# Layer 0 of a two-layer graph attention: four chunks of a tile's probabilities transposed by DMA instead of three

## The chip, the cores and the metric

The kernel runs on one core of a Trainium2 chip. The metric is the device time of one execution in microseconds (us), the median of the runs of the kernel. In the profile the engines are PE (TensorE's matmuls; PEld are its weight loads), DVE (VectorE), ACT (ScalarE), POOL (GpSimd) and SP (SyncE, which here only issues DMAs).

## The reference

Two attention layers over 6144 rows of width 128, each followed by a residual sum and a layer norm. The change is in the first of them, called layer 0 in the reference and here.

```
def _L0_gnn_ref(xx_anchor, input, adj, weight):
    anchor_adj = jnp.einsum('md,de,ne->mn', xx_anchor, weight, input)
    scores = jnp.where(adj > 0, anchor_adj, NEG_PAD)
    atten = jax.nn.softmax(scores / TEMPERATURE, axis=1)
    return atten @ input

x = _layernorm(x + _L0_gnn_ref(x, L0_gnn_input, adj, L0_gnn_weight), axis=-1)
x = _layernorm(x + _L1_gnn_ref(x, adj, L1_gnn_W, L1_gnn_a1, L1_gnn_a2), axis=-1)
```

`adj` is an int32 matrix of 6144 x 6144, `input` and `x` are float32 matrices of 6144 x 128. Layer 1 uses the same `adj` with additive scores and does not touch what is changed.

## The kernel before

**Tiles and steps.** Layer 0 works through 48 tiles of 128 rows. A tile has 6144 columns, cut in 12 chunks of 512. The kernel is a software pipeline: iteration `t` has 12 steps `c` = 0 to 11, and at step `c` the engines work on chunks of three tiles. In iteration `t`, PE makes the scores of chunk `c` of tile `t` (three matmuls of 512 columns, L574 to L576, since the operands are split into a high and a low float16 part). DVE adds the mask and keeps the maximum, a pair of chunks at a time, at odd steps (L866). ACT takes the exponential of chunk `c` of tile `t - 1` (L730). PE turns a chunk of probabilities with four float32 transposes (L563) three steps after its exponential, ACT rounds the turned chunk to float16 (`pT_hi`, L717), DVE subtracts for the low part (`pT_lo`, L875), and PE multiplies both with `vals` two steps later (L541, L543, eight matmuls). PSUM has two banks for turned chunks, so a turn waits until `pT_lo` of the turn but one before has been made; a scores matmul at an even step waits for the masked pair of three steps before.

**The moved chunks.** The first `MOVED` = 3 chunks of each tile are not turned by PE. ACT rounds them in one copy to float16 (`moved_hi`, L724, at step `c == MOVED`), POOL subtracts for the low part in one instruction (`moved_lo`, L429), and SP issues one DMA transpose for each (L352, L354). PE uses them last of the tile, in the next iteration. In the profile `moved_hi` and `moved_lo` carry the name `inp_sb`, whose space they take over. So the steps of an iteration at which a moved chunk's turn would stand (3, 4, 5) have no transposes.

**Masks.** The adjacency of a tile comes in four quarters of 1536 columns. DVE turns each into a mask `neg_mask` of zeros and large negative numbers (`make_mask`, L841); quarters 0 and 1 of tile `t + 1` are made at steps 6 and 8 of iteration `t`, quarters 2 and 3 of tile `t` at steps 0 and 2 of iteration `t`. From each mask POOL makes a byte mask for layer 1 (`edges`, L404), which SP stores. The adjacency loads of the next tile wait for the masks.

**What sets the order.** Every engine runs its instructions in the order in which the code emits them, and waits on semaphores. POOL's order in an iteration is written out in `tile_rstd`: `edges` of quarter 2, `score_cols` (two instructions on an earlier tile's result, L415 and L421), `edges` of quarter 3, `moved_lo`, `edges` of quarters 0 and 1 of the next tile, and a small power (L447). ACT adds up the product of `score_cols` at step 4 (L696), ahead of its exponential of step 5 and of `xT_hi` (L685), the rounding of the next tile's transposed rows, from which DVE makes `xT_lo` (L832).

Of the kernel before, what the change touches and what calls it, by code (L numbers as in the profile page):

```python
# [9 lines left out]
LAG = 3  # L10
PT_SLOTS = 4
PV_LAG = 2
MOVED = 3
PARTS = 8
PART_SLOTS = 4
Z_LEAD = 2
# [21 lines left out]
def build(nc, x, adj, inp, w0, w1, a1, a2, edge_rows, out):  # L38
# [17 lines left out]
    with ExitStack() as ctx:  # L56
# [37 lines left out]
        pT_lo = sb0("pT_lo", [P, PT_SLOTS, CHUNK], F16)  # L94
        MW = MOVED * CHUNK
        inp_space = inp_sb[:].bitcast(F16).rearrange("p b d -> p (b d)")
# [118 lines left out]
        vals_lo = sem("vals_lo")  # L215
# [44 lines left out]

        TURNS = C - MOVED
        ATT_STEP = LAG + PV_LAG + MOVED

# [4 lines left out]
        def turn_number(tile, bc):  # L268
            return TURNS * tile + bc - MOVED

# [7 lines left out]
        def movedT_loads(tile):  # L278
            return 32 * (tile // 2 + 1)
# [6 lines left out]
        def scores_of(known):  # L286
            return known is None or known < NB
# [19 lines left out]
        def _(sp):  # L307
# [22 lines left out]
            def load_tile(t, par, known):  # L330
                if scores_of(known) and known != 0:

                    after(sp, x_turned, t)
                    sp.dma_start(xq[:], pair_rows(x, t)).then_inc(xq_in, 16)
                    for q in range(QUARTERS):

                        after(sp, mask_set, QUARTERS * (t - 1) + q + 1)
                        sp.dma_start(adj_sb[:, q, :], pair_rows(adj, t)[:, q * QW:(q + 1) * QW]).then_inc(adj_in[q], 16)
                        store_edges(t - 1, q)
                        if q == 1 and t >= 2:  # L340
                            load_xr(t - 2)
                if t == NB:
                    for q in range(QUARTERS):
                        store_edges(t - 1, q)
                    load_xr(t - 2)
                if 2 <= t <= NB + 1:
                    tile = t - 2
                    sp.wait_ge(moved_hi_set, tile + 1)
                    if tile < 2:
                        sp.wait_ge(vals_lo, (6, 9)[tile])  # L350
                    after(sp, pv_done, C * (tile - 1))
                    sp.dma_start_transpose(movedT[:, par, 0], moved_hi).then_inc(movedT_in[par], 16)  # L352
                    sp.wait_ge(moved_lo_set, tile + 1)
                    sp.dma_start_transpose(movedT[:, par, 1], moved_lo).then_inc(movedT_in[par], 16)  # L354
                if t == NB + 1:
                    load_xr(t - 2)
# [28 lines left out]
        def _(pool):  # L385
# [37 lines left out]
            def moved_low(tile):  # L423
                pool.wait_ge(moved_hi_set, tile + 1)
                if tile == 0:
                    pool.wait_ge(vals_lo, 3)
                if tile >= 1:
                    pool.wait_ge(movedT_in[(tile - 1) % 2], movedT_loads(tile - 1))
                nc.gpsimd.tensor_tensor(moved_lo, rows[:, tile % 2 * N:tile % 2 * N + MOVED * CHUNK], moved_hi,  # L429
                                        ALU.subtract).then_inc(moved_lo_set, 1)  # L430
# [238 lines left out]
        def _(act):  # L669
# [29 lines left out]
            def tile_steps(t, par, known):  # L699
                for c in range(C):  # L700
                    if known == 0:
                        if c + Z_LEAD + 1 < C:
                            inpT_out(c + Z_LEAD + 1)
                        if c + Z_LEAD < C:
                            z_high(c + Z_LEAD)
                    if c == ATT_STEP and ends_tile(known):

                        act.wait_ge(pv_done, C * (t - 1))
                        after(act, u_set, t - 2)
                        nc.scalar.copy(att[:], ps[:, PV, 0:2 * P]).then_inc(att_out, 1)  # L710
                    if turn_at(known, c):
                        off, bc = turn_of(t, c)
                        n = turn_number(t - off, bc)
                        act.wait_ge(turned, n + 1)
                        if n >= PT_SLOTS:
                            act.wait_ge(pv_done, attend_number((n - PT_SLOTS) // TURNS, (n - PT_SLOTS) % TURNS + MOVED) + 1)
                        nc.scalar.copy(pT_hi[:, n % PT_SLOTS, :], ps[:, PT0 + n % NPT, :]).then_inc(pT_hi_set, 1)  # L717
                    if c == MOVED and 1 <= t <= NB:
                        act.wait_ge(exp_set, C * (t - 1) + MOVED)
                        if t == 1:  # L720
                            act.wait_ge(vals_lo, 3)
                        if t >= 2:
                            act.wait_ge(movedT_in[t % 2], movedT_loads(t - 2))
                        nc.scalar.copy(moved_hi, rows[:, (1 - par) * N:(1 - par) * N + MOVED * CHUNK]).then_inc(moved_hi_set, 1)  # L724
                    if known is None or 1 <= known <= NB:

                        if c == 0:
                            act.wait_ge(bias_set, t)
                            after(act, sum_set, t - 2)
                        nc.scalar.activation(row_chunk(1 - par, c), row_chunk(1 - par, c), ACT.Exp,  # L730
                                             bias=exp_bias[:, 1 - par:2 - par], scale=EXP_SCALE,
                                             accum_out=part_sum[:, 1 - par, c:c + 1]).then_inc(exp_set, 1)
                    if c == x_step(known) and (known is None or known < NB - 1):
                        xT_high(t + 1, 1 - par)
                    if c == 4 and t >= 3:
                        score_sums(t - 3)
# [76 lines left out]
        def _(dve):  # L813
# [21 lines left out]
            def make_mask(t, q, known):  # L835

                dve.wait_ge(adj_in[q], 16 * (t + 1))

                after(dve, masked, PAIRS * (t - 1) + pairs_of(q) if known != 0 else 0)
                after(dve, edges_set, QUARTERS * (t - 1) + q + 1 if known != 0 else 0)  # L840
                nc.vector.tensor_scalar(neg_mask[:, q, :], adj_sb[:, q, :], 0.0, -MASK_BIG, ALU.is_le,  # L841
                                        ALU.mult).then_inc(mask_set, 1)
# [6 lines left out]
            def tile_steps(t, par, known):  # L849
                for c in range(C):  # L850
# [27 lines left out]
                    if known == 0:  # L878
                        if c in (2, 5, 8):
                            make_mask(0, c // QC + 1, 0)  # L880
                        elif c >= C - 2:
                            make_mask(1, c - (C - 2), None)
                    else:
                        if c in (0, 2) and scores_of(known):
                            make_mask(t, 2 + c // 2, known)
                        if c in (6, 8) and (known is None or known < NB - 1):
                            make_mask(t + 1, (c - 6) // 2, None)
                    if t == 0 and c >= 5 and c % 2 == 1:
# [186 lines left out]
```

## Time and profile before

| | us |
|---|---|
| median of 3 runs | 1493.58 |
| lowest and highest | 1492.31, 1494.48 |
| the profiled execution's own time | 1494.69 |
| its span | 1492.9 |
| PE busy in the span | 1439.6 (96%) |
| DVE busy | 1326.4 (89%) |
| ACT busy | 1065.3 (71%) |
| POOL busy | 982.8 (66%) |
| DMA engines' share (the main queue) | 70.3% |

The span runs from the first to the last instruction that the profiler saw. Busy times are unions over an engine's instructions; PE's matmuls overlap, so that a busy PE says only that it did not stand still. Layer 0 takes about the first 1010 us of the span; its 48 tiles follow one another at equal distances.

### The profile page before, as it was taken

What the parts mean: (1) busy time and instruction counts of PE and PEld (TensorE: products, weight loads), DVE (VectorE), ACT (ScalarE), POOL (GpSimd) and SP (SyncE); (2) the same over time, 40 slices, a digit from 0 to 9 for tenths busy, and PEclk for the clock granted to TensorE, in tenths of its full rate; (3) what the DMA queues carried; (4) which work ended last, traced back from release to release, by engine and by line L of the source; (5) the groups of instructions that cost most, each with busy time, mean ns of one, the idle gap of its engine ahead of it and who ended that gap; (6) DMA issues with size and microseconds to landing.
All of it is one profiled execution on the core that took longest, in us unless ns stands there. A gap on an engine that the chain in (4) does not pass through costs nothing.

```text
span 1492.9 us, 28265 instructions
## 1 busy us (share of the span) xinstructions
PE 1439.6 (96%) x9853; PEld 1030.7 (69%) x9853; DVE 1326.4 (89%) x2303; ACT 1065.3 (71%) x2327; POOL 982.8 (66%) x629
## 2 busy tenths in 40 slices
PE   7799999999999999999999999987999999999996
PEld 4477777777777777777777777774566666666664
DVE  5999999999999999999999999967779797979794
ACT  4588888888888888888888888877745454546463
POOL 6455555555555555555555555527999999999995
PEclk9999999999999999999999999998999999999998
DMA  7889889888898889899989888753334343444420
GB/s 253 241 236 257 232 241 257 246 241 235 250 260 238 238 243 254 240 238 251 255 235 244 245 256 231 195 114 86 85 64 100 84 99 84 98 86 94 90 57 14
DMA packets 378766, 278.81 MB, mean 187 GB/s; under 512 B 307713, under 2 KB 354049, under 8 KB 378625
## 3 DMA queue, kind: packets, MB, share of 16 engines
q1 hardware_dynamic: 378624, 277.01, 70.3%
q8 instruction: 79, 1.29, 0.4%
q14 instruction: 63, 0.51, 0.1%
HBM read 160.56 MB, written 40.89 MB: 135 GB/s over the span
## 4 chain that ended last, share of the span: by engine, by line
PE 90%; POOL 3%; DVE 2%; issue 2%; ACT 1%; DMA 1%; SPq 0%; ACTq 0%; POOLq 0%; DVEq 0%
PE ps L541 16%; PE ps L563 13%; PE ps L623 11%; PE ps L616 10%; PE ps L543 8%; PE ps L574 8%; PE ps L576 8%; PE ps L575 8%; PE ps L600 5%; POOL p_lo L460 2%; PE ps L634 1%; DMA inp_sb<-inp 1%; ACT rows L730 1%; POOL vals_lo L456 1%; DVE rows L866 1%
## 5 line engine op out<-in xcount | busy, mean ns | idle before, releaser
L404 POOL TENSOR_SCALAR edges<-neg_mask 128x1536 uint8<-128x1536 bf16 x192 | 285.0, 1484 | 329.3 <-DVE neg_mask L841 329.0
L730 ACT ACTIVATE rows<-rows,exp_bias 128x512 f32<-128x512 f32 x576 | 415.2, 721 | 40.5 <-DVE exp_bias L933 40.5
L460 POOL TENSOR_TENSOR p_lo<-p,p_hi 128x1024 fp32r<-128x1024 f32 x180 | 426.5, 2408 | 13.2 <-PE ps L600 7.7
L960 DVE SCALAR_TENSOR_TENSOR p<-ps,e_col,edgesT 128x1024 f32<-128x1024 f32 x288 | 349.0, 1277 | 62.2 <-PE ps L593 37.5
L866 DVE CUSTOM_DVE_ANT_0 rows<-ps,neg_mask 128x1024 f32<-128x1024 f32 x288 | 351.1, 1219 | 32.3 <-PE ps L576 26.0
L717 ACT CAST pT_hi<-ps 128x512 f16<-128x512 f32 x432 | 252.1, 583 | 135.7 <-PE ps L563 127.7
L541 PE MATMUL ps<-vals,pT_hi 128*128 128x256 f16 x1728 | 331.8, 273 | 1.2 <-ACT att L710 0.8
L759 ACT CAST p_hi<-p 128x1024 fp32r<-128x1024 f32 x180 | 185.1, 1047 | 176.6 <-DVE p L960 174.4
L543 PE MATMUL ps<-vals,pT_lo 128*128 128x128 f16 x1728 | 308.6, 219 | 0.0
L875 DVE TENSOR_TENSOR pT_lo<-ps,pT_hi 128x512 f16<-128x512 f32 x432 | 287.8, 684 | 17.3 <-ACT pT_hi L717 17.3
L563 PE MATMUL ps<-ident,rows 128*128 128x128 f32 x1728 | 263.6, 275 | 7.4 <-DVE pT_lo L875 6.4
L574 PE MATMUL ps<-zT,xT_hi 128*128 128x512 f16 x576 | 219.5, 381 | 5.8 <-DVE part_max L866 4.0
L575 PE MATMUL ps<-zT,xT_hi 128*128 128x512 f16 x576 | 219.3, 381 | 0.0
L576 PE MATMUL ps<-zT,xT_lo 128*128 128x512 f16 x576 | 219.3, 381 | 0.0
L841 DVE TENSOR_SCALAR neg_mask<-adj_sb 128x1536 bf16<-128x1536 int32 x192 | 218.4, 1137 | 0.0
L541 PEld LDWEIGHTS ps<-vals,pT_hi 128*128 128x128 f16 x1728 | 169.2, 98 | 66.2 <-DVE pT_lo L875 1.9
L543 PEld LDWEIGHTS ps<-vals,pT_lo 128*128 128x128 f16 x1728 | 169.2, 98 | 49.6 <-issue 0.3
L623 PE MATMUL ps<-p,vals 128*128 128x512 f32 x432 | 203.5, 593 | 0.0
L563 PEld LDWEIGHTS ps<-ident,rows 128*128 128x128 f32 x1728 | 184.8, 142 | 19.2 <-issue 6.4
L616 PE MATMUL ps<-p_hi,vals_hi 128*128 128x512 f32 x360 | 157.3, 518 | 7.6 <-POOL vals_lo L456 5.0
L429 POOL TENSOR_TENSOR inp_sb<-rows,inp_sb 128x1536 f16<-128x1536 f32 x48 | 149.8, 3120 | 6.5 <-ACT inp_sb L724 2.7
L623 PEld LDWEIGHTS ps<-p,vals 128*128 128x128 f32 x432 | 81.4, 189 | 60.6 <-issue 52.2
(108 smaller groups left out, 1731.0 us busy)
## 6 DMA issues: line engine op xcount, KB each, us to landing
adj_sb<-adj SPq DMA_DIRECT2D x192, 768.0 KB, 5.3
edge_rows<-edges SPq DMA_DIRECT2D x192, 192.0 KB, 4.8
xq<-x SPq DMA_DIRECT2D x48, 64.0 KB, 2.6
xr<-x SPq DMA_DIRECT2D x48, 64.0 KB, 1.9
out<-y_w SPq DMA_DIRECT2D x5, 512.0 KB, 3.7
inp_sb<-inp SPq DMA_DIRECT2D x3, 768.0 KB, 10.1
inp_sb<-inp_sb SPq DMA_TRANSPOSE x96, 5.1
edgesT<-edge_rows SPq DMA_TRANSPOSE x48, 5.6
```

The source lines that it names most:

```text
L460: nc.gpsimd.tensor_tensor(p1_lo[:, m % LO_SLOTS, :], p1[:, (NB * g + n) % P_SLOTS, :], p1_hi[:, m % HI_SLOTS, :].bitcast(F32), ALU.subtrac ...
L541: nc.tensor.matmul(acc, p_hi, vals[:, jb, :], start=(bc == MOVED and b == 0), stop=False, skip_group_check=True)
L543: mm = nc.tensor.matmul(acc[:, P:2 * P], p_lo, vals[:, jb, 0:P], start=False, stop=(bc == MOVED - 1 and b == BPC - 1), skip_group_check=True)
L563: mm = nc.tensor.transpose(ps[:, PT0 + n % NPT, b * P:(b + 1) * P], rows[:, pb * N + bc * CHUNK + b * P:pb * N + bc * CHUNK + (b + 1) * P] ...
L574: nc.tensor.matmul(scores_bank(c), xT_hi[:, par, :], zT[:, 0, cols], start=True, stop=False)
L575: nc.tensor.matmul(scores_bank(c), xT_hi[:, par, :], zT[:, 1, cols], start=False, stop=False)
L576: nc.tensor.matmul(scores_bank(c), xT_lo[:, par, :], zT[:, 0, cols], start=False, stop=True).then_inc(scored, 1)
L616: mm = nc.tensor.matmul(acc_half(g % 2, i), v[:, k, :], p1_hi[:, m % HI_SLOTS, i * CHUNK:(i + 1) * CHUNK], start=(n == 0 and v is vals1_hi ...
L623: mm = nc.tensor.matmul(acc_half(g % 2, i), vals1[:, n, :], p1[:, (NB * g + n) % P_SLOTS, i * CHUNK:(i + 1) * CHUNK], start=(n == 0), stop ...
L730: nc.scalar.activation(row_chunk(1 - par, c), row_chunk(1 - par, c), ACT.Exp, bias=exp_bias[:, 1 - par:2 - par], scale=EXP_SCALE, accum_ou ...
L866: nc.vector.tensor_tensor_reduce(row_pair(par, k), scores_pair(k), neg_mask_row[:, 2 * k * CHUNK:2 * (k + 1) * CHUNK], 1.0, -3.0e38, ALU.a ...
L960: nc.vector.scalar_tensor_tensor(out=p1[:, (NB * g + n) % P_SLOTS, :], in0=ps[:, R_ROW:R_ROW + 2, :].rearrange("p b w -> p (b w)"), scalar ...
```

## The change

`MOVED` goes from 3 to 4: chunks 0 to 3 of each tile take the way over DMA, and PE has 8 chunks to turn instead of 9. `moved_hi` and `moved_lo` grow from 1536 to 2048 columns; the ACT copy stands at step 4 instead of 3. `ATT_STEP` (the step from which a tile's products with `vals` begin) is `LAG + PV_LAG + MOVED` and goes from 8 to 9, and with it go the copy of the finished sums (L710) and the small instructions of the layer norm on DVE (L908 to L921). The counts that guard the shared space of `inp_sb` are adapted. Apart from that, `make_mask` of quarters 2 and 3 stands at steps 2 and 4 instead of 0 and 2.

```diff
-MOVED = 3
+MOVED = 4
...
                     if tile < 2:
-                        sp.wait_ge(vals_lo, (6, 9)[tile])
+                        sp.wait_ge(vals_lo, MOVED * (tile + 2))
...
                 if tile == 0:
-                    pool.wait_ge(vals_lo, 3)
+                    pool.wait_ge(vals_lo, MOVED)
...
                         if t == 1:
-                            act.wait_ge(vals_lo, 3)
+                            act.wait_ge(vals_lo, MOVED)
...
-                        if c in (0, 2) and scores_of(known):
-                            make_mask(t, 2 + c // 2, known)
+                        if c in (2, 4) and scores_of(known):
+                            make_mask(t, 1 + c // 2, known)
                         if c in (6, 8) and (known is None or known < NB - 1):
                             make_mask(t + 1, (c - 6) // 2, None)
```

DVE's queue before, in steps 0 to 5 of an iteration (`x_all` is the finished row of an earlier tile; L866 is a pair of scores, its second row the reading of the maximum; the masks are quarters 2 and 3):

```order
L841 TENSOR_SCALAR neg_mask<-adj_sb 128x1536 [waits edges_set,masked,adj_in2]
L924 TENSOR_SCALAR x_all<-xr,moments,small 128x128 [waits rstd_set]
L866 ISA rows,part_max<-ps,neg_mask 128x1024 [waits max_set,scored,moved_lo_set,mask_set]
L866 ISA part_max 128x1
L875 TENSOR_TENSOR pT_lo<-ps,pT_hi 128x512 [waits pT_hi_set] x2
L841 TENSOR_SCALAR neg_mask<-adj_sb 128x1536 [waits edges_set,masked,adj_in3]
L866 ISA rows,part_max<-ps,neg_mask 128x1024 [waits turned,scored,moved_lo_set,mask_set]
L866 ISA part_max 128x1
L897 TENSOR_REDUCE small<-part_sum 128x1
L899 RECIPROCAL small<-small 128x1 [waits sum_set]
L866 ISA rows,part_max<-ps,neg_mask 128x1024 [waits scored,turned,mask_set]
```

The same place now:

```order
L924 TENSOR_SCALAR x_all<-xr,moments,small 128x128 [waits rstd_set]
L866 ISA rows,part_max<-ps,neg_mask 128x1024 [waits max_set,scored,moved_lo_set,mask_set]
L866 ISA part_max 128x1
L875 TENSOR_TENSOR pT_lo<-ps,pT_hi 128x512 [waits pT_hi_set] x2
L841 TENSOR_SCALAR neg_mask<-adj_sb 128x1536 [waits edges_set,masked,adj_in2]
L866 ISA rows,part_max<-ps,neg_mask 128x1024 [waits scored,moved_lo_set,mask_set]
L866 ISA part_max 128x1
L897 TENSOR_REDUCE small<-part_sum 128x1
L899 RECIPROCAL small<-small 128x1 [waits sum_set]
L841 TENSOR_SCALAR neg_mask<-adj_sb 128x1536 [waits edges_set,masked,adj_in3]
L866 ISA rows,part_max<-ps,neg_mask 128x1024 [waits scored,turned,mask_set]
```

The mask of quarter 2 has moved behind the pair of step 1 and the two `pT_lo` of steps 1 and 2; the one of quarter 3 stands behind the pair of step 3 and the two small instructions, where it meets the pair of step 5.

DVE's queue right behind, from the end of step 5's pair to step 8, before (the masks are quarters 0 and 1 of the next tile):

```order
L866 ISA part_max 128x1
L832 SCALAR_TENSOR_TENSOR xT_lo<-ps,xT_hi 128x128 [waits xT_hi_set]
L902 TENSOR_SCALAR small<-small 128x1 [waits inv_set]
L875 TENSOR_TENSOR pT_lo<-ps,pT_hi 128x512 [waits pT_hi_set]
L841 TENSOR_SCALAR neg_mask<-adj_sb 128x1536 [waits edges_set,masked,adj_in0]
L866 ISA rows,part_max<-ps,neg_mask 128x1024 [waits scored,turned,mask_set]
L866 ISA part_max 128x1
L875 TENSOR_TENSOR pT_lo<-ps,pT_hi 128x512 [waits pT_hi_set] x2
L841 TENSOR_SCALAR neg_mask<-adj_sb 128x1536 [waits edges_set,masked,adj_in1]
```

The same place now:

```order
L866 ISA part_max 128x1
L832 SCALAR_TENSOR_TENSOR xT_lo<-ps,xT_hi 128x128 [waits xT_hi_set]
L902 TENSOR_SCALAR small<-small 128x1 [waits inv_set]
L841 TENSOR_SCALAR neg_mask<-adj_sb 128x1536 [waits edges_set,masked,adj_in0]
L866 ISA rows,part_max<-ps,neg_mask 128x1024 [waits scored,turned,mask_set]
L866 ISA part_max 128x1
L875 TENSOR_TENSOR pT_lo<-ps,pT_hi 128x512 [waits pT_hi_set] x2
L841 TENSOR_SCALAR neg_mask<-adj_sb 128x1536 [waits edges_set,masked,adj_in1]
```

The `pT_lo` of step 6 is gone from between the small instruction and the mask of quarter 0.

POOL's queue in an iteration, from the `edges` of quarter 2, before:

```order
L404 TENSOR_SCALAR edges<-neg_mask 128x1536 [waits mask_set,edges_out2]
L415 TENSOR_TENSOR s_prod<-x_all,wa_rep 128x256 [waits s_set,wa_copied,x1_set]
L421 TENSOR_TENSOR x_total<-x_total,x_all 128x128 [waits total_set]
L404 TENSOR_SCALAR edges<-neg_mask 128x1536 [waits mask_set,edges_out3]
L429 TENSOR_TENSOR inp_sb<-rows,inp_sb 128x1536 [waits movedT_in1,moved_hi_set]
L404 TENSOR_SCALAR edges<-neg_mask 128x1536 [waits mask_set,edges_out0]
L404 TENSOR_SCALAR edges<-neg_mask 128x1536 [waits mask_set,edges_out1]
```

The same place now:

```order
L404 TENSOR_SCALAR edges<-neg_mask 128x1536 [waits mask_set,edges_out2]
L415 TENSOR_TENSOR s_prod<-x_all,wa_rep 128x256 [waits s_set,wa_copied,x1_set]
L421 TENSOR_TENSOR x_total<-x_total,x_all 128x128 [waits total_set]
L404 TENSOR_SCALAR edges<-neg_mask 128x1536 [waits mask_set,edges_out3]
L429 TENSOR_TENSOR inp_sb<-rows,inp_sb 128x2048 [waits movedT_in1,moved_hi_set]
L404 TENSOR_SCALAR edges<-neg_mask 128x1536 [waits mask_set,edges_out0]
L404 TENSOR_SCALAR edges<-neg_mask 128x1536 [waits mask_set,edges_out1]
```

Only the width of the subtraction L429 has changed in POOL's queue, from 1536 to 2048; what has moved is when the masks come that its `edges` wait for.

## Rows read from the trace of the kernel before

**Rows 1.** Busy time by stretch, 42 tiles of layer 0: engine busy us (instructions).

```profile
core 0: us, PE busy (x) PEld busy (x) DVE busy (x) ACT busy (x) POOL busy (x), PEclk, DMA share, GB/s
132.89:969.45 836.56, 836.35 (x7100) 625.62 (x7098) 795.54 (x1555) 688.41 (x1681) 449.62 (x337) 1.00 0.89 243
```

**Rows 2.** Timeline, PE, one tile: start us, us, engine, line, xcount.

```profile
500.18 0.61 PE L563 MATMUL ps<-ident,rows 128*128 128x128 f32 x4
...
501.94 0.61 PE L563 MATMUL ps<-ident,rows 128*128 128x128 f32 x4
...
510.81 0.38 PE L574 MATMUL ps<-zT,xT_hi 128*128 128x512 f16 x1
...
512.12 0.38 PE L574 MATMUL ps<-zT,xT_hi 128*128 128x512 f16 x1
```

**Rows 3.** Timeline, DVE, the same tile, [idle before <- releaser].

```profile
507.90 0.95 DVE L841 TENSOR_SCALAR neg_mask<-adj_sb 128x1536 bf16<-128x1536 int32 x1
...
511.37 1.16 DVE L841 TENSOR_SCALAR neg_mask<-adj_sb 128x1536 bf16<-128x1536 int32 x1
512.45 1.21 DVE L866 CUSTOM_DVE_ANT_0 rows<-ps,neg_mask 128x1024 f32<-128x1024 f32 x1
...
513.78 0.16 DVE L899 RECIPROCAL small<-small 128x1 f32<-128x1 f32 x1
514.41 1.23 DVE L866 CUSTOM_DVE_ANT_0 rows<-ps,neg_mask 128x1024 f32<-128x1024 f32 x1 [0.47 <-PE ps L576]
...
515.56 0.29 DVE L832 SCALAR_TENSOR_TENSOR xT_lo<-ps,xT_hi 128x128 f16<-128x128 f32 x1
515.76 0.14 DVE L902 TENSOR_SCALAR small<-small 128x1 f32<-128x1 f32 x1
...
516.71 1.46 DVE L841 TENSOR_SCALAR neg_mask<-adj_sb 128x1536 bf16<-128x1536 int32 x1
518.09 1.21 DVE L866 CUSTOM_DVE_ANT_0 rows<-ps,neg_mask 128x1024 f32<-128x1024 f32 x1
...
519.23 1.28 DVE L875 TENSOR_TENSOR pT_lo<-ps,pT_hi 128x512 f16<-128x512 f32 x2
520.43 0.94 DVE L841 TENSOR_SCALAR neg_mask<-adj_sb 128x1536 bf16<-128x1536 int32 x1
```

**Rows 4.** Timeline, POOL, the same tile.

```profile
510.57 0.73 POOL L415 TENSOR_TENSOR s_prod<-x_all,wa_rep 128x256 f32<-128x256 f32 x1
511.25 0.46 POOL L421 TENSOR_TENSOR x_total<-x_total,x_all 128x128 f32<-128x128 f32 x1
512.69 1.47 POOL L404 TENSOR_SCALAR edges<-neg_mask 128x1536 uint8<-128x1536 bf16 x1 [0.98 <-DVE neg_mask L841]
514.24 3.11 POOL L429 TENSOR_TENSOR inp_sb<-rows,inp_sb 128x1536 f16<-128x1536 f32 x1
```

**Rows 5.** Timeline, ACT, the same tile.

```profile
511.03 1.47 ACT L724 CAST inp_sb<-rows 128x1536 f16<-128x1536 f32 x1
...
513.83 0.29 ACT L696 ACTIVATE s_prod<-s_prod 128x128 f32<-128x128 f32 x1
...
515.12 0.26 ACT L685 ACTIVATE xT_hi<-ps 128x128 f16<-128x128 f32 x1
```

**Rows 6.** Timeline, POOL, near the start.

```profile
43.98 1.77 POOL L404 TENSOR_SCALAR edges<-neg_mask 128x1536 uint8<-128x1536 bf16 x1 [0.97 <-DVE neg_mask L841]
```

**Rows 7.** Timeline, DVE, near the start.

```profile
43.74 0.67 DVE L827 SCALAR_TENSOR_TENSOR vals<-inp_sb,vals 128x512 f16<-128x512 f32 x1
...
44.63 1.93 DVE L841 TENSOR_SCALAR neg_mask<-adj_sb 128x1536 bf16<-128x1536 int32 x1
```

**Rows 8.** Timeline, SP's queue, the tile of rows 3.

```profile
514.93 2.48 SPq L352 DMA_TRANSPOSE inp_sb<-inp_sb  x1
517.47 2.42 SPq L354 DMA_TRANSPOSE inp_sb<-inp_sb  x1
```

**Rows 9.** The page's DMA issues: xcount, us to landing.

```profile
inp_sb<-inp_sb SPq DMA_TRANSPOSE x96, 5.1
```

## The prediction

> **What bounds the kernel now.** I read the busy times of the long even stretch of layer 0 first, then one tile of it on each engine. 42 tiles take 836.56 us, 19.92 us each, at PE's full granted clock (1.00, the 2.4 GHz level) [rows 1]. PE stands still for only 0.2 us of all that, so PE bounds layer 0. But DVE is busy 795.54 us, 18.94 of 19.92 us per tile, and hardly has room. ACT has 3.5 us per tile to spare, POOL 9.2, and the DMA engines show a share of 0.89 [rows 1]. PE's timeline gives its prices: a step with a turn takes 501.94 - 500.18 = 1.76 us, one without 512.12 - 510.81 = 1.31 us [rows 2]. A turn costs 0.45 us.
>
> On DVE some masks are stretched. The same instruction takes 0.95, 1.16, 1.46 and 0.94 us [rows 3]. The two long ones start while POOL runs: `x_total` ends at 511.71 and `moved_lo` at 517.35 [rows 4], and the masks end at 512.53 and 518.17 [rows 3], each 0.82 us after POOL. So such a mask does next to nothing until POOL's instruction ends. POOL's `edges` does the same to it: one runs from 43.98 to 45.75 [rows 6], and the mask started at 44.63 ends at 46.56 [rows 7], 0.81 us later. It holds the other way too: that `edges` took 1.77 us instead of 1.47 [rows 4, 6] since DVE's low part of `vals` was running until 44.41 when it started [rows 7]. Whoever starts first keeps the other out. No mask of the tile shown was running when a POOL instruction started, so for this pair the second direction is inferred.
>
> The Trainium skill, page "SBUF — State Buffer", section "SBUF: two separate sides", says that DVE and GpSimd share a pair of ports under an exclusive lock, held by the one that starts first for its whole instruction. The rows above agree.
>
> **The change, part by part.**
>
> PE loses one turn per tile, 0.45 us. If nothing else held, a tile would take 19.92 - 0.45 = 19.5 us, and the kernel 48 x 0.45 = 21.6 us less: 1473 against the profiled execution's own 1494.69.
>
> DVE loses one `pT_lo`. Two take 520.43 - 519.23 = 1.20 us [rows 3], so 0.60. Without it and without the stretching (0.21 + 0.51) DVE's work is 18.94 - 0.60 - 0.72 = 17.6 us per tile. What decides is how much of the 19.5 - 17.6 = 1.9 us between them the collisions with POOL take.
>
> `moved_lo` takes 3.11 us for 1536 columns [rows 4]; from 128 columns (0.46) to 1536 the slope is 1.9 ns per column, so 2048 cost 4.1 us. `moved_hi` on ACT goes from 1.47 us [rows 5] to 1.96 at most, by a third, and a rounding of a turned chunk goes away: no price, since ACT has 3.5 us per tile.
>
> I walk DVE and POOL through the new order. Time 0 is the start of quarter 2's mask. Prices on DVE, start to start [rows 3]: mask 0.87 free, or 0.74 after POOL lets go; pair 1.14; reduction and reciprocal 0.35; `xT_lo` 0.20 and the small one 0.14; `pT_lo` 0.60. On POOL: `edges` starts 0.16 after its mask's end and takes 1.47, `s_prod` and `x_total` 1.14 together, 0.08 between two [rows 3, 4].
>
> - POOL's `edges` of quarter 2 runs from 1.11 to 2.58. DVE reaches quarter 3's mask at 2.36, is held until 2.58, goes on at 3.32. `s_prod`, due at 2.67, finds that mask running and ends at 4.0, `x_total` at 4.45; `edges` of quarter 3 runs from 4.5 to 6.0.
> - ACT adds up `s_prod` ahead of its exponential of step 5 and of `xT_hi`: start of the sums to start of `xT_hi` is 515.12 - 513.83 = 1.29 us, and `xT_hi` takes 0.26 [rows 5]. So `xT_hi` ends at 5.6. DVE, done with its pair at 4.46, waits for it, and reaches quarter 0's mask at 6.0 instead of 4.8. This mask ends its slot at 6.8.
> - `moved_lo` is due at 6.06, finds the mask running, and runs from 6.75 to 10.85. Before, it was over 517.35 - 511.37 = 5.98 us after quarter 3's mask had begun; now 8.5.
> - DVE makes a pair and two `pT_lo` and reaches quarter 1's mask at 9.14. It is held until 10.85 and leaves at 11.59.
>
> Without collisions this part of DVE's queue takes 4 masks, 3 pairs, 2 `pT_lo` and 0.69: 8.8 us. It takes 11.6: 2.8 us are lost. The rest of the tile is 17.6 - 8.8 = 8.8 us. Sum: 20.4. In that rest the two updates of `xr`, which read two operands from SBUF as the low part of `vals` does, meet POOL's delayed `edges` of quarter 1: 0.6 us more by the same walk (bounds 0 and 1.5, one whole `edges`). Sum: 21.0 us per tile, 1.1 more than 19.92. PE, with 19.5, waits for `pT_lo`: the turn of step 11 needs the one of step 9, which now comes behind the mask held longest. Over 45 tiles that is +50 us; the three others and the tail keep their 0.45: -1. Against the profiled execution's own 1494.69 us (span 1492.9) this gives 1544, and against the median, 1.1 lower, **1542 us**.
>
> The other things that move are hidden. The layer norm's instructions on DVE go one step back; the power on POOL and the exponential's bias come some 0.6 us later, and ACT has that room. The loads of quarters 2 and 3 start two steps later and are needed two steps later. The transposes: SP's issue takes 2.4 to 2.5 us each [rows 8], a third more now; before, the second was issued at 517.47 and landed about 5.1 us later [rows 9], 522.6, and PE needs it at step 5 of the next tile, 513.4 + 19.9 = 533.3 [rows 2]. Some 6 us later still fits. Adjacency loads queued behind them on SP are needed a tile later. The DMA engines: 0.89 of 19.92 is 17.7 us of work per tile, 243 GB/s x 19.92 us = 4.84 MB, of which the moved transposes are 0.79. A third more of these is 0.95 us by bytes, 1.9 if they cost double: 19.6 us at most, under DVE's time.
>
> **The rivals.**
>
> PE stays the bound (faster). It takes a POOL that is not held up by running masks, against the second direction above: the walk's POOL chain then ends 1.45 us earlier, DVE's tile comes to 19.6 with the `xr` updates and 19.0 without, PE's is 19.5. Time: 1473. Against it: the low part of `vals` does hold POOL; and 1.9 us of room against 2.8 needed.
>
> The collisions are short (no change or a little slower). If `s_prod` does not hold up ACT and only one of the two masks delays POOL, 19.9 to 20.3 us per tile: 1493 to 1511.
>
> `moved_lo` wins the race against quarter 0's mask (much slower). They come at 6.06 and 6.0, closer than I can read the walk. The mask would then be held until 10.16, the pair of step 7 start at 10.9, quarter 1's mask run freely to 14.1 and a tile take 23.5 us: 45 x 3.6 = +162, 1655. It decides from a mask 0.06 us later. If it wins in some tiles only, the time lies between. For the mask: it waits already when `edges` ends, while POOL needs 0.08 us to its next.
>
> The transfers become the bound: 19.6 us at most by the bytes, inside the first rival.
>
> **How the numbers follow.** The forecast mechanism, 1511 to 1575: 0.52. The race lost in part or wholly, 1575 to 1660: 0.2. Short collisions, 1497 to 1511: 0.08, and 1490 to 1497: 0.05. PE the bound, 1473: 0.12. Worse than 1660: 0.03. The range 1497 to 1660 holds 0.8. A measurement tells 0.2% (3 us) from no change. Faster by more: 0.13. Within it: 0.04. Slower: 0.83, by the same cases.
>
> **What would show it.** Right: steps without turns are four per tile; `moved_lo` is 4.1 us long; quarter 1's masks take about 2.5 us instead of 0.94 and end 0.8 after `moved_lo`; DVE waits for `xT_hi`; PE waits for `pT_lo` at a turn; tiles 21 us apart. Quarter 0's masks of 5 us would show the lost race. Wrong: masks all near 0.95 us and PE without gaps at 19.5 us per tile, or POOL instructions that start under a running mask and keep their usual length.

## The result

The changed kernel takes 1535.48 us (median of 4 runs, 1534.76 to 1537.93) against 1494.03 us of the kernel before (4 runs, 1492.31 to 1494.64): 1.0283 times as long, 95% interval 1.0267 to 1.0298. The forecast was 1542 us, in a range of 1497 to 1660. The profiled execution took 1534.76 us with a span of 1532.7 us, 39.8 us longer than the span before.

The busy times of the long even stretch of layer 0, in the columns of [rows 1], now read (span 1532.7 us):

```profile
132.89:969.45 836.56, 793.09 (x6642) 581.82 (x6641) 787.21 (x1450) 648.95 (x1570) 542.22 (x322) 1.00 0.88 247
```

PE, which had no gaps in [rows 1], stands still for 43.5 of 836.56 us. The turns it no longer makes have turned into waiting, and into more of it. POOL's busy time has grown from 449.62 to 542.22 us in the same stretch, though it now holds 40 tiles instead of 42; the 40 longer `moved_lo` account for 40 x 1.0 us. DMA share (0.88 for 0.89) and granted clock stay where they were.

One tile on DVE, the timeline that answers to [rows 3] (start, length, engine, line, operation; idle time before it in brackets):

```profile
509.12 0.95 DVE L841 TENSOR_SCALAR neg_mask<-adj_sb 128x1536 bf16<-128x1536 int32 x1
...
511.44 1.08 DVE L841 TENSOR_SCALAR neg_mask<-adj_sb 128x1536 bf16<-128x1536 int32 x1
...
514.73 0.29 DVE L832 SCALAR_TENSOR_TENSOR xT_lo<-ps,xT_hi 128x128 f16<-128x128 f32 x1 [1.05 <-ACT xT_hi L685]
...
515.00 0.95 DVE L841 TENSOR_SCALAR neg_mask<-adj_sb 128x1536 bf16<-128x1536 int32 x1
...
517.00 1.28 DVE L875 TENSOR_TENSOR pT_lo<-ps,pT_hi 128x512 f16<-128x512 f32 x2
518.20 2.51 DVE L841 TENSOR_SCALAR neg_mask<-adj_sb 128x1536 bf16<-128x1536 int32 x1
520.63 1.21 DVE L866 CUSTOM_DVE_ANT_0 rows<-ps,neg_mask 128x1024 f32<-128x1024 f32 x1
...
522.98 0.75 DVE L908 SCALAR_TENSOR_TENSOR xr<-att,small,xr 128x128 f32<-128x128 f32 x1
...
529.90 0.95 DVE L841 TENSOR_SCALAR neg_mask<-adj_sb 128x1536 bf16<-128x1536 int32 x1
```

Two masks of quarter 2 start at 509.12 and 529.90: a tile takes 20.78 us instead of 19.92. The mask of quarter 1 at 518.20 takes 2.51 us, where it took 0.94 in [rows 3]. DVE waits 1.05 us for `xT_hi`.

POOL in the same tile, answering to [rows 4]:

```profile
511.79 1.31 POOL L415 TENSOR_TENSOR s_prod<-x_all,wa_rep 128x256 f32<-128x256 f32 x1
...
515.15 4.74 POOL L429 TENSOR_TENSOR inp_sb<-rows,inp_sb 128x2048 f16<-128x2048 f32 x1
519.98 3.62 POOL L404 TENSOR_SCALAR edges<-neg_mask 128x1536 uint8<-128x1536 bf16 x2
```

`moved_lo` ends at 515.15 + 4.74 = 519.89, and the held mask at 518.20 + 2.51 = 520.71, 0.82 us later, the same distance as in the kernel before. And here is what the trace of before did not have: POOL instructions that started while a mask was running. `s_prod` shows 1.31 us instead of 0.73, and `moved_lo` 4.74 us, against 4.09 where it starts beside no mask (run a below). The two `edges` at 519.98 show the same once more: `moved_lo` has ended, the held mask is running, and the first of the two takes 2.06 us instead of 1.47. Together POOL is held 1.8 us per tile (0.58, 0.65 and 0.59).

Not every DVE instruction is held. In the stretch above, 120 pairs of scores and 200 `pT_lo`, which read one operand from PSUM, started while a POOL instruction was running and had 0.2 us or more to go, and kept their usual length (1.21 to 1.23 and 0.67 to 0.69 us). Held were the masks (1.08 and 2.51 us) and the first update of `xr` (0.75 instead of 0.34 us).

PE in the same tile, with the wait that the profile puts to it:

```profile
519.61 0.61 PE L563 MATMUL ps<-ident,rows 128*128 128x128 f32 x4
...
522.60 0.63 PE L563 MATMUL ps<-ident,rows 128*128 128x128 f32 x4 [1.08 <-DVE pT_lo L875]
```

From one turn to the next it is 2.99 us instead of 1.76. The turn at 522.60 (step 11) waits 1.08 us for `pT_lo` of step 9, which DVE makes behind the held mask and a pair of scores.

### The profile page after: what moved, and what is told of

It reads as the page before. It is cut to its first block, busy times and chain, and to the rows that moved or that the text cites. A ratio compares the mean times of both kernels' runs of the same rounds, so it can differ in the third digit from the quotient of the medians.

```text
span 1532.7 us, 27643 instructions
## 1 busy us (share of the span) xinstructions
PE 1430.0 (93%) x9661; PEld 1010.4 (66%) x9661; DVE 1353.4 (88%) x2255; ACT 1051.8 (69%) x2279; POOL 1112.6 (73%) x629
## 4 chain that ended last, share of the span: by engine, by line
DVE 38%; PE 30%; issue 13%; POOL 11%; ACT 5%; POOLq 0%; ACTq 0%; DVEq 0%
DVE pT_lo L875 12%; DVE rows L866 12%; PE ps L623 11%; PE ps L616 10%; DVE neg_mask L841 7%; PE ps L600 5%; POOL edges L404 4%; POOL s_prod L415 4%; POOL p_lo L460 2%; ACT rows L730 2%; DVE xr L908 2%; ACT s_prod L696 2%; PE ps L541 1%; PE ps L634 1%; DVE x_all L924 1%
## 5 line engine op out<-in xcount | busy, mean ns | idle before, releaser
L404 POOL TENSOR_SCALAR edges<-neg_mask 128x1536 uint8<-128x1536 bf16 x192 | 311.5, 1622 | 212.0 <-DVE neg_mask L841 200.6
L866 DVE CUSTOM_DVE_ANT_0 rows<-ps,neg_mask 128x1024 f32<-128x1024 f32 x288 | 351.3, 1220 | 6.7 <-PE ps L576 6.5
L717 ACT CAST pT_hi<-ps 128x512 f16<-128x512 f32 x384 | 222.2, 579 | 143.9 <-PE ps L563 143.6
L541 PE MATMUL ps<-vals,pT_hi 128*128 128x256 f16 x1536 | 295.3, 273 | 1.3 <-ACT att L710 0.8
L563 PE MATMUL ps<-ident,rows 128*128 128x128 f32 x1536 | 235.9, 276 | 57.5 <-DVE pT_lo L875 56.0
L543 PE MATMUL ps<-vals,pT_lo 128*128 128x128 f16 x1536 | 274.7, 219 | 0.0
L841 DVE TENSOR_SCALAR neg_mask<-adj_sb 128x1536 bf16<-128x1536 int32 x192 | 265.1, 1381 | 0.3 <-POOL edges L404 0.3
L875 DVE TENSOR_TENSOR pT_lo<-ps,pT_hi 128x512 f16<-128x512 f32 x384 | 250.7, 682 | 9.7 <-ACT pT_hi L717 9.6
L429 POOL TENSOR_TENSOR inp_sb<-rows,inp_sb 128x2048 f16<-128x2048 f32 x48 | 226.0, 4708 | 7.6 <-ACT inp_sb L724 3.9
L563 PEld LDWEIGHTS ps<-ident,rows 128*128 128x128 f32 x1536 | 162.5, 142 | 79.6 <-issue 71.8
L541 PE MATMUL ps<-vals,inp_sb 128*128 128x256 f16 x768 | 146.9, 273 | 0.0
```

The source lines that it names most:

```text
L404: nc.gpsimd.tensor_scalar(edge_bytes[:, q, :], neg_mask[:, q, :], 1.0 / MASK_BIG, 1.0, ALU.mult, ALU.add).then_inc(edges_set, 1)
L541: nc.tensor.matmul(acc, p_hi, vals[:, jb, :], start=(bc == MOVED and b == 0), stop=False, skip_group_check=True)
L543: mm = nc.tensor.matmul(acc[:, P:2 * P], p_lo, vals[:, jb, 0:P], start=False, stop=(bc == MOVED - 1 and b == BPC - 1), skip_group_check=True)
L563: mm = nc.tensor.transpose(ps[:, PT0 + n % NPT, b * P:(b + 1) * P], rows[:, pb * N + bc * CHUNK + b * P:pb * N + bc * CHUNK + (b + 1) * P] ...
L866: nc.vector.tensor_tensor_reduce(row_pair(par, k), scores_pair(k), neg_mask_row[:, 2 * k * CHUNK:2 * (k + 1) * CHUNK], 1.0, -3.0e38, ALU.a ...
L875: nc.vector.tensor_tensor(pT_lo[:, s, :], ps[:, PT0 + n % NPT, :], pT_hi[:, s, :], ALU.subtract).then_inc(pT_lo_set, 1)
```

## The walk against the trace

The prediction's sum was a walk through DVE's and POOL's queues from the start of quarter 2's mask. The same points in the trace of after, less 509.12:

| point | walk | trace |
|---|---|---|
| DVE reaches the mask of quarter 3 | 2.36 | 2.32 |
| it goes on behind it | 3.32 | 3.33 |
| `s_prod` ends | 4.0 | 3.98 |
| `xT_hi` ends | 5.6 | 5.57 |
| the mask of quarter 0 starts | 6.0 | 5.88 |
| DVE goes on behind it | 6.8 | 6.74 |
| `moved_lo` is due | 6.06 | 6.03 |
| `moved_lo` ends | 10.85 | 10.77 |
| DVE reaches the mask of quarter 1 | 9.14 | 9.08 |
| it goes on behind it | 11.59 | 11.51 |
| the delay of the `xr` updates | 0.6 | 0.4 |
| the tile | 21.0 | 20.78 |

## Experiments

The theory: a mask on DVE and POOL's instructions shut each other out, and this, not the transfers, the longer copy or the number of turns, took the time. The rivals: the DMA transposes of a third more data (the DMA engines or SP's queue); ACT's longer copy; DVE's wait for `xT_hi`; and, for the way to PE, whether it is DVE's whole sum or one `pT_lo` that comes too late.

The runs in one view (each in turn below; "after" is the changed kernel):

| | moved chunks | masks of quarters 2, 3 / 0, 1 at steps | else | us |
|---|---|---|---|---|
| before | 3 | 0, 2 / 6, 8 | | 1494 |
| after | 4 | 2, 4 / 6, 8 | | 1535 |
| c | 4 | 2, 4 / 6, 8 | POOL subtracts a quarter | 1475 |
| d | 4 | 2, 4 / 6, 8 | transposes of 3 chunks | 1534 |
| a | 4 | 0, 2 / 6, 8 | | 1559 |
| b | 3 | 2, 4 / 6, 8 | | 1671 |
| g | 4 | 2, 4 / 6, 8 | sums behind `xT_hi` | 1531 |
| h | 4 | 2, 4 / 6, 8 | `pT_lo` first | 1558 |
| j | 4 | 0, 2 / 6, 8 | `pT_lo` first | 1523 |
| e | 4 | 0, 2 / 4, 8 | | 1496 |
| f | 4 | 0, 2 / 4, 8 | `pT_lo` first | 1469 |
| i | 3 | 0, 2 / 4, 8 | `pT_lo` first | 1489 |

### c: POOL's subtraction cut short

```diff
-nc.gpsimd.tensor_tensor(moved_lo, rows[:, tile % 2 * N:tile % 2 * N + MOVED * CHUNK], moved_hi,
+nc.gpsimd.tensor_tensor(moved_lo[:, :CHUNK], rows[:, tile % 2 * N:tile % 2 * N + CHUNK], moved_hi[:, :CHUNK],
...
-sp.dma_start_transpose(movedT[:, par, 1], moved_lo)
+sp.dma_start_transpose(movedT[:, par, 1], moved_hi)
```

> The changed kernel with POOL's subtraction cut to 512 of its 2048 columns (left out: the low part of three of the four moved chunks; the second transpose of full size reads moved_hi instead). Port theory: moved_lo takes about 1.2 us and is over before quarter 1's mask comes; of the held time only xT_hi's 1.1 us and 0.1 stay, DVE needs 18.9 us, under PE's 19.5, and the kernel is at 1473 to 1480 us. If the transfers or the ACT copy were the cost, it stays near 1535.

Measured: 1475.45 us, 0.9881 of before (0.9866 to 0.9896). The stretch of layer 0, same columns (span 1473.5):

```profile
132.89:969.45 836.56, 835.11 (x7073) 619.25 (x7071) 761.45 (x1540) 689.69 (x1672) 424.13 (x341) 1.00 0.92 257
```

PE is without gaps again, the tile takes 19.52 us (two masks of quarter 2 at 519.20 and 538.72), and that with all the transfers and the long copy of the changed kernel: the DMA share is even higher, 0.92. One instruction of POOL was shortened (and the second transpose reads `moved_hi`, at full size), and 60 us are gone. `xT_hi`'s wait of 1.05 us is still there 31 times in 600 us and costs nothing.

### d: the transposes cut short

```diff
-sp.dma_start_transpose(movedT[:, par, 0], moved_hi)
+sp.dma_start_transpose(movedT[:, par, 0, 0:12], moved_hi[:, 0:12 * P])
...
-p_hi = movedT[:, t_of % 2, 0, jb, :] if by_dma else pT_hi[:, s, cols]
+p_hi = movedT[:, t_of % 2, 0, jb % 12, :] if by_dma else pT_hi[:, s, cols]
```

(and the same for the low part)

> The changed kernel with both DMA transposes cut to three of the four chunks (left out: the transposed fourth chunk; PE reads the first one's blocks in its place). Everything on the engines is as in the changed kernel. Port theory: no difference to the changed kernel, 1535 us within 3. Transfer theory (DMA engines or SP's queue the bound): back to the transfers of before and so PE's 19.5 us per tile, 1473 to 1490.

Measured: 1534.3 us (1533.71 to 1535.01), 1.0274 of before (1.0259 to 1.029). The DMA share fell from 0.88 to 0.80 and the time by 1 us. The transfers have no part in the loss.

### a: four moved chunks, masks where they were

```diff
-                        if c in (2, 4) and scores_of(known):
-                            make_mask(t, 1 + c // 2, known)
+                        if c in (0, 2) and scores_of(known):
+                            make_mask(t, 2 + c // 2, known)
```

> Four moved chunks, but the masks of quarters 2 and 3 at steps 0 and 2 as before. Port theory (a DVE mask and a POOL instruction shut each other out): moved_lo starts some 2.9 us after quarter 3's mask and runs 4.1 us, so quarter 0's mask at step 6 comes under it and is held about 2.3 us, while quarter 1's is free; DVE's tile is 17.6 + 2.5 held + up to 0.5 of waiting = 20.1 to 20.6 us, the kernel 1502 to 1525 us, likeliest 1513. If the moving of the masks were the whole cost, this kernel would show PE's gain: 1473. If the longer transfers or the longer ACT copy were the cost, it would stay at 1535.

Measured: 1559.15 us, 1.0441 of before (1.0425 to 1.0457). The direction of the port theory, but 46 us more than its likeliest value and outside its interval. DVE's timeline, the held mask; POOL's, `moved_lo` with no mask running when it starts; and PE's, the turn that waited (span 1558.0):

```profile
506.04 3.43 DVE L841 TENSOR_SCALAR neg_mask<-adj_sb 128x1536 bf16<-128x1536 int32 x1
509.39 1.21 DVE L866 CUSTOM_DVE_ANT_0 rows<-ps,neg_mask 128x1024 f32<-128x1024 f32 x1
...
510.53 1.28 DVE L875 TENSOR_TENSOR pT_lo<-ps,pT_hi 128x512 f16<-128x512 f32 x2
```

```profile
504.56 4.09 POOL L429 TENSOR_TENSOR inp_sb<-rows,inp_sb 128x2048 f16<-128x2048 f32 x1
```

```profile
511.36 0.63 PE L563 MATMUL ps<-ident,rows 128*128 128x128 f32 x4 [1.75 <-DVE pT_lo L875]
```

The mask was held as computed (3.43 us instead of 0.95, so 2.5). What the expectation left out is the way to PE: `pT_lo` of step 7 stands behind the held mask and the pair, and the turn of step 9 needs it. The expectation had added up DVE's work; the tile is 21.3 us since PE stood still 1.75 us for one late `pT_lo`, and then DVE waited for PE's scores in its turn (20.2 us busy of 21.3, the held time counted as busy).

### b: three moved chunks, masks moved

```diff
-                        if c in (0, 2) and scores_of(known):
-                            make_mask(t, 2 + c // 2, known)
+                        if c in (2, 4) and scores_of(known):
+                            make_mask(t, 1 + c // 2, known)
```

(the change to the kernel before)

> Three moved chunks as before, only the masks of quarters 2 and 3 at steps 2 and 4. Port theory: moved_lo (3.1 us) is due about 6.1 us after quarter 2's mask starts; quarter 0's mask now has a pT_lo ahead of it and comes at 6.5, so it loses the race and is held till 9.2; with the wait for xT_hi (1.2 us) DVE's tile is 18.2 + 0.1 + 1.2 + 2.6 = 22.1 us, the kernel about 1590 us (1560 to 1610), slower than with four moved chunks. If four moved chunks were the cost (their transfers, the longer copy), this kernel would be at 1494, and at 1473 + 21 = 1494 too if the masks' place did not matter.

Measured: 1671.03 us, 1.1184 of before (1.1165 to 1.1202). The slowest of all, with PE's and the transfers' work of the kernel before. Its mask of quarter 0 loses the race that the changed kernel's wins. DVE, then POOL, then PE (span 1669.3):

```profile
505.88 0.69 DVE L875 TENSOR_TENSOR pT_lo<-ps,pT_hi 128x512 f16<-128x512 f32 x1
506.49 3.28 DVE L841 TENSOR_SCALAR neg_mask<-adj_sb 128x1536 bf16<-128x1536 int32 x1
```

```profile
505.84 3.11 POOL L429 TENSOR_TENSOR inp_sb<-rows,inp_sb 128x1536 f16<-128x1536 f32 x1
```

```profile
511.66 1.09 PE L563 MATMUL ps<-ident,rows 128*128 128x128 f32 x4 [2.68 <-DVE pT_lo L875]
512.54 0.63 PE L574 MATMUL ps<-zT,xT_hi 128*128 128x512 f16 x1
```

`moved_lo` started 0.65 us ahead of the mask; DVE went on at 509.69. The expectation had the hold and its place, and 81 us too little, outside its interval. Most of what it lacked is the clock. PE's granted clock in the wait, right behind it and after that (columns as in [rows 1]):

```profile
508.90:511.66 2.76, 0.08 (x3) 0.03 (x1) 2.76 (x5) 0.31 (x2) 1.52 (x2) 0.99 0.94 181
511.66:515.06 3.40, 3.40 (x15) 2.26 (x16) 2.17 (x3) 1.30 (x3) 1.47 (x1) 0.51 0.95 237
515.06:524.10 9.04, 9.04 (x79) 6.87 (x78) 7.99 (x21) 6.54 (x16) 0.56 (x1) 1.00 0.41 155
```

Behind the stretch without matmuls the granted clock is 0.51, the 1.2 GHz level: the four transposes take 1.09 us instead of 0.61, a scores matmul 0.63 instead of 0.38. The run itself has the comparison: through the long stretch, four tiles of five have such a time at half clock and take 24.0 to 24.3 us; every fifth has none, at the same wait of 2.68 us, and takes 22.76. So the low clock costs 1.2 to 1.6 us in a tile that has it, 1.1 on the mean of all, and the mean tile is 23.9 us, 1.8 more than the expected 22.1. The other 0.7 us stand in the tiles at full clock too; DVE waits there 0.49 us for PE's scores at step 1, which the expectation had not in its sum, and the rest was not followed up. In the changed kernel, with waits of 1.08 us, and in a, with 1.75, the mean over the stretch is 1.00.

### g: the sums behind `xT_hi`

```diff
-                    if c == 4 and t >= 3:
+                    if c == 5 and t >= 3:
                         score_sums(t - 3)
```

> The changed kernel with ACT's sums of s_prod at step 5 behind xT_hi instead of at step 4. DVE's wait for xT_hi of 1.05 us per tile goes. Port theory: it changes nothing, since quarter 0's mask then comes 1.2 us earlier and is held by edges of quarter 3 until about the same time (5.95 us after quarter 2's mask started, measured now: it starts at 5.88): quarter 0's mask shows 1.9 to 2.2 us instead of 0.95, time 1535 within 4. If the wait for xT_hi were worth its length, 45 x 1.05 = 47 us less: 1488.

Measured: 1531.08 us (1530.36 to 1531.3), 1.0251 of before (1.0237 to 1.0265), 4.4 us less than the changed kernel, against 47 if the wait were worth its length. DVE's masks of quarters 0 and 1 (span 1529.2):

```profile
511.64 2.02 DVE L841 TENSOR_SCALAR neg_mask<-adj_sb 128x1536 bf16<-128x1536 int32 x1
...
515.93 2.49 DVE L841 TENSOR_SCALAR neg_mask<-adj_sb 128x1536 bf16<-128x1536 int32 x1
```

The wait of 1.05 us is gone and its place is taken by POOL's `edges`: the mask of quarter 0 now takes 2.02 us instead of 0.95; quarter 1's mask, at the end of the chain, takes 2.5 us as before. The wait for `xT_hi` was covered: the time is within the 4 us that the expectation allowed.

### h: `pT_lo` ahead of the pair, in the changed kernel

```diff
+                    if turn_at(known, c):
+                        ...
+                        nc.vector.tensor_tensor(pT_lo[:, s, :], ps[:, PT0 + n % NPT, :], pT_hi[:, s, :],
+                                                ALU.subtract).then_inc(pT_lo_set, 1)
                     if scores_of(known) and c % 2 == 1:
                         ...
-                    if turn_at(known, c):
-                        ...
```

> The changed kernel with pT_lo ahead of the pair of scores at odd steps on DVE. It asks how the held mask reaches PE. If by the turn of step 11, which waits 1.08 us for pT_lo of step 9 behind the pair (1.14 us), that wait ends, and what is left is DVE's own sum: 17.6 of work, 1.7 held by POOL in quarter 1's mask, 0.1 in quarter 3's, 0.4 in xr, 1.05 waiting for xT_hi, together 20.8, the same as measured: DVE alone is the bound and the time stays at 1525 to 1536. If PE's stall by the order of pT_lo is the bound and DVE is not, 45 x 1.08 = 49 us less: 1487.

Measured: 1557.94 us, 1.0431 of before (1.0416 to 1.0445): slower than either answer. The tile is 21.29 us, 0.51 more. On DVE there is one new wait, at step 1 (span 1554.9):

```profile
516.52 0.34 DVE L923 TENSOR_SCALAR x_all<-xr,moments,small 128x128 f32<-128x128 f32 x1
517.36 0.69 DVE L860 TENSOR_TENSOR pT_lo<-ps,pT_hi 128x512 f16<-128x512 f32 x1 [0.50 <-ACT pT_hi L717]
```

There DVE used to make the pair while ACT, held up by the late `exp_bias`, was still at `pT_hi`; now it stands 0.50 us, and the tile is longer by just that. Meanwhile PE's wait at step 11 went down from 1.08 to 0.71 us, and gained nothing; another of 0.57 us came up at the turn of step 2. So in the changed kernel DVE's chain is what closes: its work, what POOL holds it, and its waits; PE only follows. The expectation's first answer had this right and had not looked for what the swap costs at step 1. The swap changes the order at every odd step, so this run doesn't show what it is worth at step 9 alone.

### j: the same swap in a

The edit is h's, in a.

> a_masks_0_2 (1559 us, 21.3 us per tile) with pT_lo ahead of the pair at odd steps. In a, PE waits 1.75 us at the turn of step 9 for a pT_lo that stands behind the held mask and a pair, and DVE is busy 20.2 us per tile. If PE's local wait set a's time, the pair's 1.14 us come off and DVE's sum takes over, 20.2 us plus the 0.5 that h lost at step 1: 20.7, 1533 us (1520 to 1545). If DVE's sum had set it already, nothing changes or it is 0.5 us per tile slower as h was: 1558 to 1582.

Measured: 1522.99 us (1521.78 to 1523.6), 1.0192 of before (1.0177 to 1.0208), 36 us less than a, as expected for the case that PE's wait set a's time. The held mask is still 3.43 us; the tile went from 21.3 to 20.56 us. In a the late `pT_lo` did set the time, which is the term that a's expectation lacked.

### e: the mask of quarter 0 two steps earlier

```diff
-                        if c in (2, 4) and scores_of(known):
-                            make_mask(t, 1 + c // 2, known)
-                        if c in (6, 8) and (known is None or known < NB - 1):
-                            make_mask(t + 1, (c - 6) // 2, None)
+                        if c in (0, 2) and scores_of(known):
+                            make_mask(t, 2 + c // 2, known)
+                        if c in (4, 8) and (known is None or known < NB - 1):
+                            make_mask(t + 1, (c - 4) // 4, None)
```

> Four moved chunks, masks of quarters 2 and 3 at steps 0 and 2 as before, the next tile's quarter 0 at step 4 (before: 6), quarter 1 at 8. Port theory: quarter 0's mask starts ahead of moved_lo, at the end of POOL's edges (held 0.2 us), moved_lo follows it from about 0.7 us later and is over (4.1 us) when quarter 1's mask comes at step 8; held time 0.4 to 0.6 us, DVE 18.2 us per tile, PE the bound at 19.5: 1474 us (1470 to 1480), faster than both. If the turned chunk's saving were taken back by something else (transfers, ACT's longer copy), it would stay above 1490.

Measured: 1496.26 us, 1.0018 of before (1.0009 to 1.0027): 39 us less than the changed kernel, and still 22 above the expectation. DVE's masks, POOL's `edges` of quarter 0, and the turn that waited (span 1495.3):

```profile
515.48 1.08 DVE L841 TENSOR_SCALAR neg_mask<-adj_sb 128x1536 bf16<-128x1536 int32 x1
...
520.98 1.88 DVE L841 TENSOR_SCALAR neg_mask<-adj_sb 128x1536 bf16<-128x1536 int32 x1
```

```profile
515.83 4.67 POOL L429 TENSOR_TENSOR inp_sb<-rows,inp_sb 128x2048 f16<-128x2048 f32 x1
520.58 1.47 POOL L404 TENSOR_SCALAR edges<-neg_mask 128x1536 uint8<-128x1536 bf16 x1
```

```profile
504.83 0.63 PE L563 MATMUL ps<-ident,rows 128*128 128x128 f32 x4 [0.37 <-DVE pT_lo L875]
```

The races at steps 4 and 8 against `moved_lo` went as meant. But behind `moved_lo` comes the `edges` of quarter 0, which had been due since 516.7, and it starts 0.40 us ahead of the mask of quarter 1 and holds it for 1.07 us. The expectation followed the long instruction and forgot the one queued behind it. PE waits 0.37 us at the turn of step 11, which comes 2.29 us after the turn of step 10 (502.54) instead of 1.75, and the tile is 19.92 us. At 1496 the run also lies above the 1490 that the expectation gave to another cause, the transfers or ACT's longer copy taking the saving back. f, with the same transfers and the same copy, rules that out.

### f: both

e with h's swap.

> As e_mask_at_4, and DVE makes pT_lo of an odd step ahead of the step's pair of scores instead of behind it. PE is at its own work of 19.5 us per tile in e already, so this gives nothing: 1474 us within 3 of e. If e still has PE waiting for pT_lo, f takes that back (up to 0.2 us per tile, 9 us).

Measured: **1469.49 us** (1469.19 to 1470.72), 0.9841 of before (0.9828 to 0.9854), the fastest of all. The stretch of layer 0, then its masks (span 1467.5):

```profile
132.89:969.45 836.56, 833.61 (x7122) 623.32 (x7120) 797.57 (x1546) 695.83 (x1691) 532.21 (x342) 1.00 0.99 258
```

```profile
514.46 0.95 DVE L841 TENSOR_SCALAR neg_mask<-adj_sb 128x1536 bf16<-128x1536 int32 x1
...
520.45 1.08 DVE L841 TENSOR_SCALAR neg_mask<-adj_sb 128x1536 bf16<-128x1536 int32 x1
...
525.82 2.02 DVE L841 TENSOR_SCALAR neg_mask<-adj_sb 128x1536 bf16<-128x1536 int32 x1
...
533.94 0.95 DVE L841 TENSOR_SCALAR neg_mask<-adj_sb 128x1536 bf16<-128x1536 int32 x1
```

The mask of quarter 1 is still held in 33 of the stretch's 42 tiles, 2.02 us long here, but `pT_lo` of step 9 comes right behind it instead of behind a pair, and PE has no wait at a turn in the tile shown. PE's tiles are 19.35 us apart, its own work (the two masks of quarter 2 shown are 19.48 apart; DVE makes up for it by a shorter distance in every fourth or fifth tile). Two missed expectations meet here: e lost more than the 9 us written down for it, 0.54 us per tile at the turn of step 11, and the swap, harmful in the changed kernel, takes it all back (27 us). The DMA share is 0.99 in this kernel; whether the transfers would be the next bound, no run shows.

### i: f with three moved chunks

> f_low_first (1469.5 us) with three moved chunks instead of four: the masks' and pT_lo's new order is kept. If f's gain is the turn that PE saves, this kernel has 48 x 0.45 = 21.6 us more, 1491 us (1488 to 1495), near the kernel before: the reordering alone gives it at most the 0.1 us per tile that PE waits at a turn there. If the reordering were the gain, it would be near 1470.

Measured: 1489.0 us (1488.47 to 1489.26), 0.9965 of before (0.9953 to 0.9978). 19.5 us more than f: the fourth moved chunk is worth that once no collision reaches PE (the prediction's price gives 48 x 0.45 = 21.6; PE's tiles are 19.79 us apart here and 19.35 in f). The new order alone gives 5 us.

## Why the prediction was right, and where it was off

**What bounds.** PE without gaps and DVE with one us to spare was the right reading: c shows PE's 19.5 us per tile as soon as the collision is gone (19.52). Not all of that is PE's work, though: f has 19.35, and i, with three moved chunks, 19.79 where the kernel before had 19.92. In the kernel before, one turn per tile started 0.1 us late (the one at 507.28 comes 0.15 us after the matmul ahead of it, the others 0.06), which a busy time does not show. It made no difference to this forecast, since DVE set the tile.

**The lock.** That a mask under a POOL instruction ends 0.82 us after it, and that this would meet the mask of quarter 1, came out to 0.1 us. The second direction was inferred from another DVE instruction; `s_prod` with 1.31 us and `moved_lo` with 4.74 show it for masks. Both held instructions end 0.15 us earlier than their full length behind the mask would have them.

**The race.** The mask of quarter 0 started at 515.00, `edges` ended at 515.07, and `moved_lo` was due at 515.15. The walk gave the mask 0.06 us of lead and the trace 0.15, and it was won in all tiles of the stretch (no mask of quarter 0 over 0.95 us). The prediction had said that it couldn't read so close, so that it fell on this side was in part luck. That the rival was real, and its price not small, b shows: there it is lost, and the tile is 22.8 us before the clock takes more.

**The size.** The tile was put at 21.0 us and is 20.78. The term that was mis-sized is the `xr` updates' (0.6, measured 0.4, 0.75 us for 0.34 at 522.98). The walk up to quarter 1's mask was 0.08 too long, and the rest of the tile, put at 8.8 us, took 0.07 more, so that these two cancel. Over the kernel, 45 x (20.78 - 19.92) = 39 us; the span grew by 39.8, 39.5 of it by the end of layer 0's last product. The 1 us that the prediction took off for the other tiles and the tail was not there.

**The term xT_hi.** In the sum it stood as if DVE lost it before quarter 0's mask. g shows that it was not worth its 1.05 us, but 0.1: `edges` would have held the mask in its place. The prediction's bound for this (the mask cannot start before `edges` ends at 6.0) gives the same number, so the total was not hurt. The wait itself was computed as 5.6 - 4.46 = 1.14 us and is 1.05.

**The rivals.** The rival of no loss (1473) needed POOL not to be held up; it is out. So are the short collisions: `s_prod` did hold up ACT and both masks delayed POOL. The transfers' rival is out by d, and c. (SP's issues did not grow by a third each, as the prediction had it: they take 3.14 and 1.72 us in the tile shown, after 2.48 and 2.42.) The range's upper end belonged to the lost race.

**What the prediction did not see** is how near PE stood to a wait of its own. In the changed kernel DVE's chain sets the tile, by h; in a and e PE's late `pT_lo` set it. The expectations of a, e and b, which summed DVE's queue without PE's waits, then missed by 46, 22 and 81 us.

## What to carry to other kernels

When an engine with 5% to spare shares a port with one that has long instructions, look at which instruction stands under which, not at busy shares: the sum of one tile through both queues, from the rows' start-to-start times, gave the result to 0.5%. It does so only where the engine summed is the one that sets the tile: add up the waits of the next engine too. Before moving a step, follow what is queued behind the long instruction; in e and f it was the second in the queue that held the mask. Where the bound engine waits for a product that stands behind a held instruction and something else, putting that product first gained 36 us (j) and 27 (f). The same swap cost 22 us in the changed kernel (h), where it opened a wait at another step; no run made it at the one step alone.

## What the runs showed of the hardware

A DVE mask (int32 to bfloat16 in SBUF, 1536 columns, 0.95 us) held by POOL ends 0.81 to 0.82 us after POOL's instruction, whether that is a subtraction of two operands (519.89 to 520.71 here) or a scaling of one [rows 6, 7]. The Trainium skill, page "SBUF — State Buffer", section "SBUF: two separate sides", has the rule: of a DVE instruction in a two-port mode or with two operands in SBUF, and a GpSimd instruction, whoever starts first keeps the shared ports for its whole length. Both directions agree now, and so do the pairs and `pT_lo`, which have one operand in PSUM and were never lengthened. In which mode the masks run, no run shows. The price of a hold stands in these rows. The hold shows as a longer busy time of the held instruction, on POOL (1.31 for 0.73) as on DVE, and nowhere as a wait; so POOL's share rose from 54% to 65% in the long stretch, where, over 40 tiles, the longer `moved_lo` are 40 us of work and the held time is 73 us. The profile's chain of work that ended last shows it better than the shares of busy time (PE 93%, DVE 88%, POOL 73%): where PE had 90% of the chain before, it reads now

```profile
DVE 38%; PE 30%; issue 13%; POOL 11%; ACT 5%; POOLq 0%; ACTq 0%; DVEq 0%
```

PE's waits of 1.08 us per tile left the granted clock at 1.00 in the even stretch. Behind waits of 2.68 us (b) it fell to the 1.2 GHz level in four tiles of five, and not in the fifth. In a, with waits of 1.75 us, it stayed at 1.00 but for one tile: behind its longest wait, 2.03 us (the turn at 318.06), it was 0.50 from 318.75 to 322.17, and that tile took 23.2 us instead of 21.3. So the same wait may or may not be followed by the low clock. That was not expected, and no run here changes the wait alone.
